# Units 8 to 15 added in PSUM by TensorE, the gathers issued ahead of unit 7, weight pairs loaded one per tile, six row buffers

## What is computed

```python
x = _layernorm(x + attention(x))                       # (16, 256, 256)
x = hidden_states.reshape(-1, H)                       # 4096 tokens, H = 256
topk_w, topk_ids = _grouped_topk(x @ gate_w, bias)     # 6 of 64 experts per token
se = flat_e[order]; pos = ...; valid = pos < CAP       # CAP = 2 * (256 * 6 // 64) = 48 rows per expert
h = silu(einsum('ech,ehf->ecf', buf, w_gate)) * einsum('ech,ehf->ecf', buf, w_up)
out = einsum('ecf,efh->ech', h, w_down)                # (64, 48, 256), 96 inner channels
y = segment_sum(out[se, pos] * valid * w, tok)
shared = silu(x @ ws_gate) * (x @ ws_up) @ ws_down     # 96 inner channels
x = _layernorm(x + y + shared)
```

## Time and profile before

| | us |
|---|---|
| median of three runs | 1367.67 (1365.44 to 1372.23) |
| the profiled execution | 1362.8 |
| its span, first to last instruction | 1361.0 |
| TensorE busy in the span | 1291.1 (95%) |
| VectorE, ScalarE, GpSimd busy | 1029.9, 927.8, 493.1 |
| attention and routing, to about | 1176 |
| indices to last scatter's issue | 1207.9 to 1306.6 |
| loads of the end to the end of the span | 1310.6 to 1361.0 |

### The profile page before, as it was taken

One profiled execution on the slowest core, in us unless ns is written; L12 is line 12 of the kernel. 1 busy time (PEld: TensorE's weight loads), 2 busy tenths in 40 slices (PEclk: granted clock), 3 DMA queues, 4 the chain that ended last, 5 costly groups with the idle time before them and its releaser, 6 DMA issues.

```text
span 1361.0 us, 39593 instructions
## 1 busy us (share of the span) xinstructions
PE 1291.1 (95%) x15260; PEld 1102.1 (81%) x15260; DVE 1029.9 (76%) x2327; ACT 927.8 (68%) x1746; POOL 493.1 (36%) x422
## 2 busy tenths in 40 slices
PE   7999999999999999999999999999999999978970
PEld 5788888888888888888888888888888888865550
DVE  6677878787878787888878787888787888753227
ACT  7667777777777677777777777777777777533434
POOL 0224233424232333324233423242333423335756
PEclk9999999999999999999999999999999999979995
DMA  8700000001000000000000000000000016558665
GB/s 297 261 2 10 27 9 27 9 3 32 2 26 9 26 10 26 9 27 9 26 9 27 9 13 23 10 26 17 27 17 26 17 38 197 158 170 244 107 195 203
DMA packets 47198, 81.11 MB, mean 60 GB/s; under 512 B 4464, under 2 KB 29136, under 8 KB 46160
## 3 DMA queue, kind: packets, MB, share of 16 engines
q1 hardware_dynamic: 37968, 65.58, 14.5%
q0 software_dynamic: 4608, 7.08, 3.0%
q10 hardware_dynamic: 4480, 6.29, 1.3%
HBM read 56.26 MB, written 22.68 MB: 58 GB/s over the span
## 4 chain that ended last, share of the span: by engine, by line
PE 85%; DVE 5%; DMA 4%; issue 3%; ACT 2%; POOL 1%; ACTq 0%; SPq 0%; DVEq 0%; POOLq 0%
PE pA L558 25%; PE pB L558 24%; PE pO L657 12%; PE pC L643 10%; PE pS L620 10%; DMA sums<-sb_stage,sb_sidx 3%; PE pC L558 1%; PE pS L558 1%; DVE sb_W L1195 1%; DVE sb_nmr L1654 1%; PE pC L682 1%; ACT sb_W L1174 0%; DVE sb_W L1642 0%; ACT sb_W L898 0%; POOL sb_stage L1738 0%
## 5 line engine op out<-in xcount | busy, mean ns | idle before, releaser
L1684 POOL TENSOR_TENSOR sb_vl<-sb_v,sb_vh 128x512 f16<-128x512 f32 x121 | 153.9, 1272 | 680.4 <-ACT sb_vh L944 680.4
L558 PE MATMUL pB<-sb_xh,sb_W 128*128 128x256 f16 x2048 | 349.6, 273 | 0.0
L1246 DVE TENSOR_TENSOR sb_S<-pS,sb_D 128x1024 f32<-128x1024 f32 x248 | 236.0, 952 | 120.5 <-PE pS L620 120.5
L952 ACT ACTIVATE sb_Shl<-sb_S 128x1024 f16<-128x1024 f32 x242 | 204.3, 844 | 110.9 <-DVE sb_S L1246 109.6
L558 PE MATMUL pB<-sb_xl,sb_W 128*128 128x256 f16 x1024 | 279.3, 273 | 0.0
L1252 DVE TENSOR_TENSOR sb_Shl<-sb_S,sb_Shl 128x1536 f16<-128x1536 f32 x121 | 225.4, 1863 | 10.4 <-ACT sb_Shl L952 10.1
L558 PEld LDWEIGHTS pB<-sb_xh,sb_W 128*128 128x128 f16 x2048 | 200.2, 99 | 22.8 <-issue 0.4
L558 PE MATMUL pA<-sb_xh,sb_W 128*128 128x256 f16 x1024 | 175.8, 274 | 10.2 <-DVE sb_W L1195 5.6
L558 PE MATMUL pA<-sb_W,sb_xh 128*128 128x256 f16 x1024 | 177.0, 275 | 3.7 <-ACT sb_qh L919 3.7
L657 PE MATMUL pO<-sb_Wo,sb_yh 128*128 128x256 f16 x1016 | 173.3, 273 | 0.0
L958 ACT ACTIVATE sb_gt<-pB 128x512 f32<-128x512 f32 x128 | 76.4, 597 | 140.9 <-PE pB L558 140.9
(11 more groups left out here) (290 smaller groups left out, 2711.9 us busy)
## 6 DMA issues: line engine op xcount, KB each, us to landing
sb_stage<-wprep SPq DMA_DIRECT2D x7, 1280.0 KB, 7.0
sb_W<-sums SPq DMA_DIRECT2D x16, 512.0 KB, 10.5
sb_W<-w_experts SPq DMA_DIRECT2D x17, 384.0 KB, 3.8
gather_rows<-sb_xr SPq DMA_DIRECT2D x16, 320.0 KB, 2.4
sb_xs<-xT SPq DMA_DIRECT2D x16, 256.0 KB, 2.9
sb_D<-decay SPq DMA_DIRECT2D x8, 512.0 KB, 7.9
sb_xn<-x SPq DMA_DIRECT2D x16, 256.0 KB, 3.0
sums<-sb_xr SPq DMA_DIRECT2D x16, 256.0 KB, 2.2
```

What stands on the lines that cost most here:

```text
L558: last = nc.tensor.matmul(dst, a, m, start=(i == 0), stop=(i == len(terms) - 1), **kw)
L952: nc.scalar.activation(Sh[:, :, a:z_], S[:, :, a:z_], ACT.Copy).then_inc(s_Sh, 1)
L1246: nc.vector.tensor_tensor(scores_at(h)[:, :, a:z_], pS[:, :, a:z_], d[:, :, 0:z_ - a], ALU.mult).then_inc(s_Sm, 1)
L1684: nc.gpsimd.tensor_tensor(vl[q % 2][:, :, :], v32[:, :, :], vh[q % 2][:, :, :], ALU.subtract).then_inc(s_vl, 1)
```

## The change

- Units 8 to 15 are no longer copied out of PSUM. The gate-up products of these units go to banks `pA` and `pO`, the down products (`late_down`) to eight banks of their own (`pLate`), and when a chunk's load has landed TensorE adds both regions to the bank by multiplying them with the identity (`add_sums`). VectorE takes the statistics of these chunks from PSUM, and ScalarE scales them from there. `unit_keep`, the tiles `late_sh` and GpSimd's additions are gone. All late `unit_inner` stand ahead of ScalarE's first chunk.
- VectorE makes the products of units 7 to 11, GpSimd the others. So no unit stands ahead of the gathers that comes after the indices. The count of the last sequence, its evacuation, two fills, the spreads and VectorE's last x1 split change places. Two spreads run ahead of the tiles and four inside.
- Weight pair `p` from 21 on waits for tile `p - 18` (or for the old condition, if that is later).
- The two transposed-token buffers that lay in the staging tile move to `x1T`, which frees the place for six row buffers `wo` in place of four.

```diff
-OUTBUF = 4
+OUTBUF = 6
-        xgT = carve(P, 2, NC * P)
-        xgT = [xgT[:, 0, :], xgT[:, 1, :]] + [v32[:, t, :] for t in range(NT)]
+        xgT = [x1T[:, t, :] for t in range(NC)] + [v32[:, t, :] for t in range(NT)]
+        pLateGU = [pA, pO]
+        pLate = [pB, pC] + [pS[:, i, :] for i in range(4)] + [pA, pO]
+        BY_DVE = range(UNITS_AHEAD - 1, UNITS_AHEAD + 4)
+        def whole_rows(c, k):
+            if c >= UNITS_AHEAD:
+                return pLate[c - UNITS_AHEAD][:, k * HID:(k + 1) * HID]
+            return fin[c][:, 0, k, :]
...
-                sp.wait_ge(s_md, KINDS * ((p - RING) // 4 + 1))
+                sp.wait_ge(s_md, max(KINDS * ((p - RING) // 4 + 1), p - 18))
...
+            def late_down(j):
+                pe.wait_ge(*shared_product(j))
+                pe.wait_ge(s_uact, j + 1)
+                for k in range(FIN):
+                    last = nc.tensor.matmul(pLate[j - UNITS_AHEAD][:, k * HID:(k + 1) * HID], us[0:FF, j % 2, k:T:FIN], wsd[:, :],
+                                            start=(k == 0), stop=False, skip_group_check=True)
+                last.then_inc(s_udn, 1)
+            def add_sums(c):
+                pe.wait_ge(s_fl[c], 16)
+                for k in range(FIN):
+                    for r in range(REGIONS):
+                        last = nc.tensor.matmul(pLate[c - UNITS_AHEAD][:, k * HID:(k + 1) * HID], ident[:, :], fin[c][:, r, k, :],
+                                                start=False, stop=(r == REGIONS - 1), skip_group_check=True)
+                last.then_inc(s_fp, 1)
...
@@ TensorE, behind attention @@
             unit_gate_up(4)
-            unit_down(3)
             pe.wait_ge(s_th, SEQS)
             count(SEQS, STEPS)
+            unit_down(3)
...
+            for c in range(UNITS_AHEAD, FINALS):
+                add_sums(c)
@@ ScalarE @@
             unit_store(2)
+            running_counts(SEQS)
             unit_inner(4)
             unit_store(3)
-            running_counts(SEQS)
...
-            for j in range(UNITS_AHEAD, UNITS_AHEAD + 4):
-                unit_inner(j + 1)
-                unit_keep(j)
+            for j in range(UNITS_AHEAD, SEQS):
+                unit_inner(j)
@@ VectorE @@
-            for n in range(3):
-                spread_equals(n)
             last_low_x1()
+            spread_equals(0)
+            unit_product(UNITS_AHEAD - 1)
+            spread_equals(1)
...
+            for j in range(UNITS_AHEAD, UNITS_AHEAD + 4):
+                unit_product(j)
@@ GpSimd @@
-            for j in range(1, UNITS_AHEAD):
+            for j in range(1, UNITS_AHEAD - 1):
                 unit_product(j)
...
-            for j in range(UNITS_AHEAD, UNITS_AHEAD + 5):
-                unit_product(j)
+            unit_product(UNITS_AHEAD + 4)
+            unit_product(UNITS_AHEAD + 5)
             for c in range(FINALS + 2):
-                if UNITS_AHEAD <= c < FINALS:
-                    pool.wait_ge(s_fl[c], 16)
-                    pool.wait_ge(s_uev, c + 1)
-                    nc.gpsimd.tensor_tensor(fin[c][:, 1, :, :], fin[c][:, 1, :, :], late_sh[c - UNITS_AHEAD], ALU.add).then_inc(s_fp, 1)
...
-                    j = UNITS_AHEAD + 5 + i
+                    j = UNITS_AHEAD + 6 + i
```

More of the change, by code:

```diff
@@ L391, in block_kernel, with shared_product @@
         HALVES = [(0, T), (T, T + P)]
+        BY_DVE = range(UNITS_AHEAD - 1, UNITS_AHEAD + 4)
+        def shared_product(j):
+            if j in BY_DVE:
+                return s_usd, j - BY_DVE.start + 1
+            return s_ush, len([i for i in range(j + 1) if i not in BY_DVE])
         def has(g):
@@ L712, in unit_gate_up @@
                 wait(pe, s_uact, j - 1)
-                bank = pGU[j % 2]
+                bank = (pGU if j < UNITS_AHEAD else pLateGU)[j % 2]
                 for s in range(2):
@@ L794, in _ @@
             unit_gate_up(6)
+            unit_down(5)
             pe.wait_ge(s_ids, 1)
@@ L866, in _ @@
                     transpose_tokens(p + 1)
-                n = p + 3
+                n = p + 2
                 if n < TILES // EQB:
-                    pe.wait_ge(s_eq, n * EQB)
+                    pe.wait_ge(s_eq, (n if n > 2 else 1) * EQB)
                     spread_ids(n)
@@ L991, in unit_store @@
                 act.dma_start(shared_t[j], ue[j % UEV].rearrange("p (t n) -> p t n", t=NT)).then_inc(s_ust[j % UEV], 16)
-            def unit_keep(j):
-                act.wait_ge(s_udn, j + 1)
-                if j == UNITS_AHEAD:
-                    for i in range(UEV):
-                        act.wait_ge(s_ust[i], 16 * (UNITS_AHEAD // UEV))
-                nc.scalar.activation(late_sh[j - UNITS_AHEAD], pUD[j % 2][:, :].rearrange("p (k n) -> p k n", k=FIN),
-                                     ACT.Copy).then_inc(s_uev, 1)
             def normed(b):
@@ L1122, in evacuate @@
                 act.wait_ge(s_mT, t + 1)
+                if t == 0:
+                    act.wait_ge(s_x1l, SEQS)
                 wait(act, s_mgu, t + 1 - KINDS)
@@ L1173, in _ @@
                 for k in range(FIN):
-                    last = nc.scalar.activation(fin[c][:, 1, k, :], fin[c][:, 0, k, :], ACT.Identity,
+                    last = nc.scalar.activation(fin[c][:, 1, k, :], whole_rows(c, k), ACT.Identity,
                                                 scale=frs[:, c % FACT, k:k + 1], bias=nmr[:, c % FACT, k:k + 1])
@@ L1659, in _ @@
                 if c < FINALS:
-                    dve.wait_ge(s_fadd, c + 1)
+                    if c < UNITS_AHEAD:
+                        dve.wait_ge(s_fadd, c + 1)
+                    else:
+                        dve.wait_ge(s_fp, c - UNITS_AHEAD + 1)
                     for k in range(FIN):
-                        last = nc.vector.bn_stats(st6[:, c % 2, k, :], fin[c][:, 0, k, :])
+                        last = nc.vector.bn_stats(st6[:, c % 2, k, :], whole_rows(c, k))
                     last.then_inc(s_fst, 1)
```

43 lines of the change are left out of this document (17 added, 26 removed).

## The result

The changed kernel takes 1351.51 us (median of 4, 1350.25 to 1355.0), the kernel before beside it 1366.74 us (median of 4, 1365.44 to 1372.23). The ratio is 0.9885 with a 95% interval of 0.9852 to 0.9918: 15.2 us faster. The forecast was 1343 with a range of 1333 to 1356: the range and the sign hold, the gain is under two thirds of the one forecast. The profiled execution took 1355.0 us (span 1353.2), 3.5 us over its median, and that of before lay 4.9 under its own; so the two traces are only 7.8 us apart.

A forecast was written before the change was run, and what follows sets the result against it. It took GpSimd's scatters to pace the tile loop and VectorE to bound the end. Gains of 7.6 + 5.1 + 0 + 11.8 = 24.5 us off the median of 1367.67 gave 1343 us, range 1333 to 1356.

The forecast's parts named there:

- The front, (1): In front of the tiles: indices at 1207.0, tile 0 at 1213.0, scatter 2 7.6 us sooner (bounds 6 and 10).
- Scatters 2 to 15, (2): Tile loop: weight pairs loaded one per tile make this stretch 47.1 us against 52.2, a gain of 5.1 us.
- Scatters 15 to 23, (3): Last tiles: 18.9 us, set by the scatters' own latency and the way to the next issue; unchanged, 0.
- The end, (4): Final stage: DMA becomes the bound, 31 us of transfers plus 7.6 behind, 38.6 against 50.4, gaining 11.8 us.
- The lower clock: Rival, final stage: TensorE's sums stay at 3.8 us a chunk, the stage gains nothing, 1355 us; chance 0.12.
- The sum: Whole kernel: 7.6 + 5.1 + 0 + 11.8 = 24.5 us gained, forecast 1343 us from the median.
- slow scatters: Rival, tile loop: spread loads don't quicken the scatters, so scatters 2 to 15 gain nothing, 1348 us; chance 0.17.
- The buffers: Rival, tile loop: copies, not the scatter rule, stalled it; up to 7 us more gained, 1336 us; chance 0.09.
- Slower than before: Rival, tile loop: loads beside every tile hold all scatters at the worst latency, eating 19.4 us; chance 0.02.

The follow-up runs named there:

- chips B and C: Second and third of the three chips used for follow-up runs, four runs on each; the kernel before takes 1366.70 and 1367.17 us there.
- semaphore last: The changed kernel with its one new semaphore allocated behind all others: 1335.56 us on chip A (ratio 0.9818), 1352.87 us on chip B (0.9895).
- chip A: First of the three chips used for follow-up runs, four runs on it; the kernel before takes 1361.06 us there.
- end mixed: The changed kernel with the final chunks in another order (0 to 4, 8, 5, 9, 6, 10, 7, 11 to 15): 1352.49 us on chip C, ratio 0.9893.
- the end alone: The kernel before with only the final stage changed (units 8 to 15 in PSUM, both regions added by TensorE): 1350.08 us on chip A, ratio 0.9908.
- pairs by four: The changed kernel with weight pairs released four at a time, as before: 1348.74 us on chip B (ratio 0.9865), 1349.59 us on chip C (0.9868).

## Why the prediction was right or wrong

The trace of before on which every term was worked out has no late release; the changed kernel's trace has 17, and the times beside the trace of before (1365.44 to 1372.23 us) are like those of chips B and C, which have them. So I go through the steps twice: against the trace of the change with its semaphore last on chip A, where the conditions are those of the rows, and against the measured case.

**The front, (1).** The working holds link by link on chip A. The indices are ready at 1205.55 there and tile 0 is on TensorE at 1211.41: 5.9 us, for the 6.0 forecast (1207.0 to 1213.0). To scatter 0 7.4 us (1218.85) for 7.5, to scatter 2 7.1 (1225.94) for 7.4. In the trace of the changed kernel itself gather 0 is issued at 1207.65 and tile 0 transposed at 1213.21, right to 0.5 us. Then the late releases set in, with these two of ScalarE:

```profile
1213.21 0.41 PE L841 MATMUL pA<-sb_ident,sb_stage 128*128 128x128 f32 x2 [0.73 <-issue]
...
1217.88 0.25 ACT L1162 ACTIVATE sb_yh<-pB 128x96 f32<-128x96 f32 x1 [3.83 <-remote]
...
1220.76 0.27 ACT L1169 ACTIVATE sb_qh<-pC 96x128 f32<-96x128 f32 x1 [2.35 <-remote]
```

Scatter 0 comes 13.2 us behind tile 0, and scatter 2 1.8 us earlier than before for the 7.6 forecast. Most of that 5.8 is the wrong trace for the comparison: between two traces of chip C, before and with its end mixed, scatter 2 moves from 1240.35 to 1232.95, 7.4 us.

**Scatters 2 to 15, (2).** Forecast 47.1 for 52.2 us. Chip A 45.2 (1225.94 to 1271.14), the changed trace 48.5, chip C 48.1 for 52.4. The gain of 3.7 to 7.0 us lies about the 5.1 forecast; spread loads did quicken the scatters (51.9 to 44.5 us on chip A, above), and that rival is out. The account holds on chip A alone, where the scatters lag behind the copies (below) and wait only 5.8 us for them. On the others TensorE and no longer the DMA sets the pace: the scatters of the changed trace wait 19.1 us for copies. The copies' own idle time doesn't tell the two apart, for with six buffers it is all TensorE's on chip A too (29.6 us).

**Scatters 15 to 23, (3): the step that failed.** "Unchanged, 0 (bounds -1 and +1)". On chip A it is so, 18.5 us (1271.14 to 1289.67) for 18.9. On the others it is 24.95 in the changed trace and 24.9 for 18.3 on chip C: 6.0 to 6.7 us lost. The prediction took it that TensorE would run two tiles further ahead of the scatters. Before, it did run ahead: its copy 15 is at 1278.85 and scatter 15 at 1287.71, 8.9 us behind it, and a late release only eats into time in which VectorE's next copy would have waited for a scatter anyway. In the kernel before on chip C, with as many of them, the copies wait 24.6 us for scatters, for the 35.9 of the earlier trace rows, and the tiles take the same 78.0 us (lines from 1175 us on):

```profile
L1621 DVE COPY sb_stage<-pS 128x256 f32<-128x256 f32 x24 | 10.2, 425 | 42.0 <-DMA sums<-sb_stage,sb_sidx 24.6 <-PE pS L855 15.4 <-issue 2.0
```

The changed kernel without late releases keeps the lead. On chip A copy 15 and scatter 15 are 8.5 us apart (timelines of VectorE and GpSimd):

```profile
1262.66 0.43 DVE L1645 COPY sb_stage<-pS 128x256 f32<-128x256 f32 x1 [1.09 <-PE pS L883]
...
1271.14 1.59 POOL L1772 DMA_INDIRECT sums<-sb_stage,sb_sidx  x1 [0.30 <-issue]
```

With late releases copies 0 to 15 take 55.8 us (1225.14 to 1280.97) for 45.1 on chip A, while spread loads let the scatters go on faster than before, and the lead is gone: scatter 15 is issued 1.2 us after its copy. TensorE's chain with ScalarE is now the bound, each late release on it counts, and nothing is stored up that the last eight scatters could work off at 2.4 us apiece. The tiles take 80.7 us from scatter 0 to 23 in the changed trace. With the semaphore last, one program on two chips, it is 81.3 on B (1224.92 to 1306.24) and 70.8 on A.

**The end, (4).** Forecast 38.6 for 50.4 us from the first load. Chip A 39.85 (1293.75 to 1333.6), and with the end alone 39.9; the changed trace 42.1. The form is confirmed too, by the end of the chain on chip A:

```profile
1309.91 15.30 DMA sb_W<-sums
1325.26 2.01 PE pO L754 x8
```

The last load is issued at 1309.91 and lands 15.30 us later, 31.5 us after the first was issued (forecast 31), and 8.4 us are behind it (forecast 7.6). The lower clock was the rival, and it came for one chunk of eight. TensorE's additions in the changed trace:

```profile
1327.49 3.37 PE L753 MATMUL pB<-sb_W,sb_ident 128*128 128x256 f32 x8 [2.01 <-DMA sb_W<-sums]
1331.00 1.99 PE L753 MATMUL pC<-sb_W,sb_ident 128*128 128x256 f32 x8
1333.21 1.99 PE L753 MATMUL pS<-sb_W,sb_ident 128*128 128x256 f32 x8 [0.22 <-DMA sb_W<-sums]
1335.69 1.99 PE L753 MATMUL pS<-sb_W,sb_ident 128*128 128x256 f32 x8 [0.49 <-DMA sb_W<-sums]
```

3.37 us for the first chunk, at a granted clock of 0.58 (1327.4 to 1330.9) after 2.01 us of idle time, then 1.99 each at 1.00, in spite of a short wait for a load before most of them. On chip A the first took 3.77. (The prediction's 3.8 does not follow from its row, which gives 2 x 2.07 = 4.1.) The Trainium skill, "TensorE: Matmul & The Clock Gate", section "HAM oscillation — how this bites in real kernels", describes bursts of products that each wait longer for their data than they run, and each start at the lower clock. Here the later bursts ran 1.99 us and waited 0.2 to 0.5, so this was not its case, as the prediction had taken it to be; gaps of that length did not bring the lower clock. On VectorE the 1.06 us row is gone: the instruction takes 0.13 to 0.16 us for all late chunks, and ScalarE's chunks come 1.4 to 2.5 us apart (forecast 1.6 to 2).

**The sum.** On chip A 9.6 + 7.0 + 0.4 + 10.4 = 27.4 us between its span of 1333.6 and the 1361.0 of the trace of before, some 1.5 us of it from indices that are ready that much earlier there than forecast. By the times it is 25.5, with the forecast at 24.5. With late releases it is 11.8 to 15.2. The prediction was a right account of a chip on which its kernel wasn't timed. That 1351.5 us lies in its range all the same is luck: the range was made for the lower clock and for slow scatters, and late releases were no rival of it. A warning was in the table of times, a trace 4.9 us under the median, and I took that for scatter and shifted the forecast by it as a constant. It was not a constant of the chip. Between chips without and with late releases the kernel before differs by 6 us (1366.7 and 1367.2 for 1361.1) and the changed one, with its semaphore last on both, by 17 (1352.9 for 1335.6). The traces say where. Between tile 0 and scatter 0 both lose, 5.3 us (14.2 for 8.85) and 6.5 (13.9 for 7.4); in the tiles the kernel before loses nothing and the changed one 10.5 (81.3 for 70.8). These 10.5 us are about what the forecast lacks (24.5 against 11.8 to 15.2).

**The other rivals.** The buffers: six for four are worth 1.8 us on chip A, and the two intervals overlap, so this can't be told from nothing; with four, scatter 23 is at 1290.88 for 1289.67. Slower than before: nowhere.

**What stays open.** Why pairs by four are 3 to 6 us faster where releases are late. Its late releases are no fewer in sum (16.1 us on chip B for 14.9 and 17.5). They fall otherwise, since the scatters lag behind TensorE again (7.5 us at tile 15) and GpSimd's issues no longer start at the same point of each tile; TensorE's copies 0 to 15 take 52.3 us in it (1223.8 to 1276.05) for 56.3 with the semaphore last beside it, so the same sum of late releases holds TensorE up less; that it is hit at less critical points is argued, and no run isolates it. Open too is which resource TensorE's release and GpSimd's issue share, why chip A is free of it, and whether it is the chip at all or the time at which it was used.

## What to carry to other kernels

Where a change speeds up a lagging consumer, and it comes to keep step with its producer, the slack that hid the producer's own delays is gone: before crediting such a change, list the waits of the producer's chain, and ask what each costs once nobody is behind. Late releases cost the kernel before nothing in its tiles, and the changed one 10.5 us there. And when a profile's own time lies well off the median of the times, look for what differs between them before shifting a forecast by the gap.
